# Experts stage: GpSimd issues the gathers of the tile two ahead in front of the accumulating transfers, from the last tile of 512 on

## The chip, the cores and the metric

The kernel runs on one core of one Trainium2 chip. The metric is the device time of one execution in microseconds (us). It is read from the median of three runs. The core has five engines that each run their own list of instructions in order and meet at semaphores: TensorE (PE, with its weight loads as PEld), VectorE (DVE), ScalarE (ACT), GpSimd (POOL) and SyncE (SP), and 16 DMA engines that carry all transfers.

## The reference

One decoder layer on x of 16 sequences by 256 tokens by 256, in float32. Three parts follow one another, each added to its input and normalised: a linear attention with decay, a cross attention over a context of 77 rows, and a mixture of experts. Only the last one matters here:

```
x = layernorm(x + ffn(x))          # the layer's last step, 4096 tokens of 256

probs = softmax(xf @ router_w.T)   # 8 experts
probs = probs * (top 2 of them)    # and divided by their sum
g = xf @ gate_w[e] + gate_b[e]     # 256 -> 512, per expert e
u = xf @ up_w[e] + up_b[e]
h = silu(g) * u
y = sum over e of probs[e] * (h @ down_w[e] + down_b[e])   # 512 -> 256
```

## The kernel before

The kernel runs five stages, with a barrier behind each: linear_attention, cross_attention, route_tokens, run_experts, combine. The routing stage gives every pair of a token and one of its two experts a slot, sorted by expert. The slots are cut into tiles, each with a single expert: 16 big tiles of 512 slots (BIGS = 16, tiles 0 to 15), then 7 half tiles of 256 (tiles 16 to 22), 23 in all (TILES). A tile is handled in blocks of 128 rows: 4 blocks in a big tile, 2 in a half tile. The last half tiles are the same code with 256 columns.

In run_experts each engine walks over the tiles with its own function tile(t, par, turn), where par is t % 2 and picks one of two buffers, and turn is t // 2. Tiles 0 and 1 are written out, tiles 2 to 13 run in a hardware loop (there t is a register, not an int), and 14 to 22 are written out again (all_tiles, L1779). What one tile does, by engine:

- SyncE (L1827) loads the weights of tile t + 2 into gu_raw and dn_raw, 0.5 MB each for gate, up and down, once the low parts of tile t are made, and the biases of t + 1.
- GpSimd (L1880) does three things in order. low_parts(t + 1) waits until ScalarE has made gu_hi of tile t + 1 and subtracts it from the first half of the raw weights to give that half of gu_lo. add_rows(t - 1) waits until the output rows of t - 1 are scaled (y_scaled) and until the accumulating transfers of t - 2 have landed (y_stored), then issues one indirect DMA per block that adds y_out to rows of sum_dram. gather_rows(t + 2) waits for index_ready of t + 2 and issues one indirect DMA per block that fetches the token rows into x_in.
- TensorE (L2122) begins a tile when x_lo and both halves of gu_lo for it are there. It multiplies by gate and up for f = 0 and 1 of the four blocks of 128 hidden columns (gate_up), then does the down projection of tile t - 1 (down), then turns the gathered rows of tile t + 1 (turn_x, which waits for x_loaded, the gathers), then f = 2 and 3. Each product is three matmuls, since both operands are split into a high and a low part.
- ScalarE (L1914) makes gu_hi of t + 1 from the raw weights, the gates with silu, the scaled output rows of t - 1 (scale_y), xT_hi of t + 1 from the turned rows, dn_hi and hid_hi.
- VectorE (L2025) makes hid, keeps the rows of t - 1 (keep_y, which waits for the accumulating transfers of t - 3 through y_stored), makes the other half of gu_lo of t + 1 (gu_low_last, L1997), xT_lo (x_low), the shares of t + 1 (shares), and then the index of tile t + 2 (tile_index, L2019), which waits for turn_x and shares of tile t. So index_ready of t + 2 comes behind x_low of t + 1, and that behind the transposes of t + 1.

The order on GpSimd is written out by hand in tile; there is no planner. Both kinds of indirect DMA are issued by GpSimd's instruction stream.

Of the kernel before, what the change touches and what calls it, by code (L numbers as in the profile page):

```python
# [1462 lines left out]
class Plan:  # L1463
# [29 lines left out]
    def blocks(self, t):  # L1493

        return (self.T if not isinstance(t, int) or t < self.BIGS else self.HALF) // P

    def first_block(self, t):

        if not isinstance(t, int) or t <= self.BIGS:
            return t * (self.T // P)  # L1500
        return (self.BIGS * self.T + (t - self.BIGS) * self.HALF) // P
# [203 lines left out]
def run_experts(nc, sh, plan, ident, x2_dram, slot_col, slot_row, counts, expert_of, tile_table, gate_w, gate_b, up_w, up_b, down_w, down_b, sum_dram):  # L1705
# [8 lines left out]
    T, BIGS, TILES = plan.T, plan.BIGS, plan.TILES  # L1714
# [5 lines left out]
    with ExitStack() as ctx:  # L1720
# [58 lines left out]
        def all_tiles(eng, tile):  # L1779

            for t in range(2):
                tile(t, t, 0)
            with eng.Fori(1, (BIGS - 2) // 2) as i:
                for par in range(2):
                    tile(2 * i + par, par, i)
            for t in range(BIGS - 2, TILES):
                tile(t, t % 2, t // 2)

        def has(t, ahead):

            return not isinstance(t, int) or 0 <= t + ahead < TILES
# [59 lines left out]
        @block.gpsimd  # L1851
        def _(pool):

            def gather_rows(t, par, turn):
                pool.wait_ge(index_ready[par], turn + 1)
                pool.sem_inc(pool_turns, 1)
                for blk in range(blocks(t)):
                    pool.indirect_dma_start(x_in[par][:, blk, :], None, x2_dram,  # L1858
                                            bass.IndirectOffsetOnAxis(index[par][:, blk:blk + 1], 0))\
                        .then_inc(x_loaded[par], 16)  # L1860

            def low_parts(par, turn):
                pool.wait_ge(gu_hi_done[par], turn + 1)
                pool.sem_inc(pool_turns, 1)
                for cols in (slice(0, FF), slice(FF, 2 * FF)):
                    ins = pool.tensor_tensor(gu_lo[par][:, 0, cols], gu_raw[par][:, 0, cols],
                                             gu_hi[par][:, 0, cols].bitcast(F32), ALU.subtract)
                ins.then_inc(gu_lo_done[par], 1)

            def add_rows(t, par, turn):  # L1870
                pool.wait_ge(y_scaled, first_block(t + 1))
                pool.wait_ge(target_ready, t + 1)
                if has(t, -1):
                    pool.wait_ge(y_stored[1 - par], 16 * plan.blocks_of_parity(t - 1, turn - 1 + par))
                pool.sem_inc(pool_turns, 1)
                for blk in range(blocks(t)):
                    pool.indirect_dma_start(sum_dram, bass.IndirectOffsetOnAxis(target[par][:, blk:blk + 1], 0),  # L1877
                                            y_out[par][:, blk, :], None, compute_op=ALU.add).then_inc(y_stored[par], 16)

            def tile(t, par, turn):  # L1880
                if has(t, 1):
                    low_parts(1 - par, turn + par)
                if has(t, -1):
                    add_rows(t - 1, 1 - par, turn - 1 + par)
                if has(t, 2):
                    gather_rows(t + 2, par, turn + 1)

            gather_rows(0, 0, 0)
            gather_rows(1, 1, 0)
            all_tiles(pool, tile)  # L1890
            add_rows(TILES - 1, (TILES - 1) % 2, (TILES - 1) // 2)

# [406 lines left out]
```

## Time and profile before

| | us |
|---|---|
| median of 3 runs | 1451.87 |
| the three runs | 1449.99, 1451.87, 1453.0 |
| the profiled execution | 1452.94 |
| its span, first to last instruction | 1450.9 |
| TensorE busy | 1315.6 (91%) |
| TensorE weight loads busy | 1115.7 (77%) |
| ScalarE busy | 953.5 (66%) |
| VectorE busy | 833.1 (57%) |
| GpSimd busy | 745.7 (51%) |
| mean granted TensorE clock | 0.953 |

The profile is of one execution. Busy times are sums over instructions, and a matmul's end is modelled, so a busy TensorE is not TensorE at its peak. Times within the span are counted from its first instruction. PEclk is the clock that the chip granted to TensorE, as a share of full speed. A releaser is what ended an engine's idle time, inferred from semaphores. The first gather of the experts stage starts at 1030.0 and the last accumulating transfer at 1417.2; the combine stage follows from 1423.3 to the end. "Landing" is the time from the start of the instruction that issues a transfer to its completion.

### The profile page before, as it was taken

The numbers are of one execution on the slowest core, as the hardware profiler recorded it, in microseconds if no ns is written. First come the engines' busy times: TensorE is split into PE (matmuls) and PEld (weight loads), VectorE is DVE, ScalarE is ACT, GpSimd is POOL, SyncE is SP. The second block draws the span as 40 slices with busy tenths as digits, with TensorE's granted clock in tenths as the row PEclk, the third lists the DMA queues.
The fourth block names the chain that finished last, engine by engine and source line by source line (L and its number), as shares of the span: only waits on it lengthen the run. The fifth ranks groups of instructions, "written<-read, shape, count | busy, mean of one in ns | idle before, by whom it ended". The sixth has DMA issues, their size and how long they took to land. (4 is left out here: it accounts for less than half of the span.)

```text
span 1450.9 us, 31123 instructions
## 1 busy us (share of the span) xinstructions
PE 1315.6 (91%) x10437; PEld 1115.7 (77%) x10437; DVE 833.1 (57%) x1707; ACT 953.5 (66%) x2168; POOL 745.7 (51%) x841
## 2 busy tenths in 40 slices
PE   5899999999999999999988999982599999999780
PEld 4788888888888888888876777761488888888680
DVE  3345554445454455544556888857366666666564
ACT  4577767777777777777745777772466666656553
POOL 2244443444444444443547777740357777776753
PEclk9999999999999999999999999995599999999895
DMA  3300100001000100010023343422346666666737
GB/s 138 82 9 30 31 23 25 21 23 31 23 31 16 30 24 30 24 37 9 23 80 86 107 104 98 112 83 72 113 136 153 153 155 154 155 157 163 180 78 239
DMA packets 136851, 117.54 MB, mean 81 GB/s; under 512 B 46578, under 2 KB 121690, under 8 KB 136730
## 3 DMA queue, kind: packets, MB, share of 16 engines
q1 hardware_dynamic: 121754, 95.36, 21.6%
q0 software_dynamic: 14976, 20.62, 8.1%
q8 instruction: 70, 1.15, 0.3%
q14 instruction: 51, 0.42, 0.1%
HBM read 79.89 MB, written 33.58 MB: 78 GB/s over the span
## 5 line engine op out<-in xcount | busy, mean ns | idle before, releaser
L345 POOL TENSOR_SCALAR_AFFINE_SELECT a_decay<-a_decay 128x256 f32<-128x256 f32 x256 | 115.2, 454 | 258.2 <-ACT a_decay L433 256.7
L565 DVE TENSOR_TENSOR a_probs<-a_ps_s,a_decay 128x384 f32<-128x384 f32 x256 | 131.6, 552 | 158.5 <-PE a_ps_o L752 147.4
L354 POOL TENSOR_TENSOR a_key_sum<-a_probs 128x256 f32<-128x256 f32 x128 | 94.5, 738 | 169.9 <-DVE a_probs L565 157.9
L1877 POOL DMA_INDIRECT sum_rows<-e_y_out,e_target x78 | 125.8, 1613 | 81.0 <-ACT e_y_out L1931 56.5
L396 ACT ACTIVATE a_qk_exp<-a_ps_qk 128x512 f32<-128x512 f32 x128 | 76.5, 598 | 137.2 <-PE a_ps_qk L658 130.0
L658 PE MATMUL a_ps_qk<-a_xT_hi,a_w_hi 128*128 128x256 f32 x512 | 144.8, 283 | 3.6 <-ACT a_qk_relu L397 3.6
L658 PE MATMUL a_ps_qk<-a_xT_hi,a_w_lo 128*128 128x256 f32 x512 | 143.8, 281 | 0.0
L658 PE MATMUL a_ps_qk<-a_xT_lo,a_w_hi 128*128 128x256 f32 x512 | 143.7, 281 | 0.0
L558 DVE SCALAR_TENSOR_TENSOR a_qk<-a_qk_exp,a_qk_relu 128x512 f32<-128x512 f32 x128 | 89.1, 696 | 94.5 <-ACT a_qk_relu L397 94.3
L733 PE MATMUL a_ps_s<-a_qk 64*128 64x256 f32 (+1 forms) x1024 | 132.2, 338 | 0.6 <-DVE a_probs L565 0.5
L431 ACT ACTIVATE a_decay<-a_ps_c,a_c_now 128x256 f32<-128x256 f32 x256 | 124.4, 486 | 2.1 <-PE a_ps_c L723 1.2
L1858 POOL DMA_INDIRECT e_x_in<-x_rows,e_index x78 | 81.1, 1039 | 79.1 <-DVE e_index L2023 56.0
L746 PE MATMUL a_ps_o<-a_probs,a_values 128*64 128x256 f32 (+1 forms) x1024 | 111.5, 339 | 0.4 <-DVE a_probs L565 0.4
L733 PEld LDWEIGHTS a_ps_s<-a_qk 64*128 64x128 f32 x1024 | 107.8, 187 | 2.5 <-issue 2.4
L658 PEld LDWEIGHTS a_ps_qk<-a_xT_hi,a_w_hi 128*128 128x128 f32 x512 | 97.8, 191 | 5.7 <-issue 5.6
L433 ACT ACTIVATE a_decay<-a_ps_c,a_c_now 128x128 f32<-128x128 f32 x256 | 98.4, 385 | 0.0
L658 PEld LDWEIGHTS a_ps_qk<-a_xT_hi,a_w_lo 128*128 128x128 f32 x512 | 98.0, 191 | 0.0
L658 PEld LDWEIGHTS a_ps_qk<-a_xT_lo,a_w_hi 128*128 128x128 f32 x512 | 97.8, 191 | 0.0
L359 POOL TENSOR_TENSOR a_oT_lo<-a_oT,a_oT_hi 128x256 fp32r<-128x256 f32 x128 | 94.4, 738 | 1.2 <-ACT a_oT_hi L450 1.2
L746 PEld LDWEIGHTS a_ps_o<-a_probs,a_values 128*64 128x64 f32 x1024 | 62.2, 136 | 41.5 <-issue 11.3
L1036 POOL TENSOR_TENSOR b_probs<-b_probs,b_top 128x1232 f32<-128x1232 f32 x32 | 72.7, 2273 | 39.8 <-DVE b_top L1231 39.8
L2119 PE MATMUL e_ps_y<-e_dn_hi,e_hid_hi 128*128 128x256 f32 x312 | 89.0, 285 | 3.1 <-DVE e_hid_lo L2039 2.2
(318 smaller groups left out, 4017.2 us busy)
## 6 DMA issues: line engine op xcount, KB each, us to landing
e_gu_raw<-in_L_ffn_gate_w SPq DMA_DIRECT2D x23, 512.0 KB
e_gu_raw<-in_L_ffn_up_w SPq DMA_DIRECT2D x23, 512.0 KB
e_dn_raw<-in_L_ffn_down_w SPq DMA_DIRECT2D x23, 512.0 KB, 5.3
a_x_in<-in_x SPq DMA_DIRECT2D x16, 256.0 KB, 2.7
a_x_res<-in_x SPq DMA_DIRECT2D x16, 256.0 KB
x_rows<-a_x SPq DMA_DIRECT2D x16, 256.0 KB, 2.2
x_bo_rows<-a_x_bo SPq DMA_DIRECT2D x16, 256.0 KB, 2.2
b_x_bo<-x_bo_rows SPq DMA_DIRECT2D x16, 256.0 KB, 2.9
```

The lines of the kernel that those rows point to most:

```text
L345: pool.affine_select(out=d, in_=d, compare_op=ALU.is_ge, fill=0.0, base=0, pattern=[[0, 2], [1, P]], channel_multiplier=-1)\
L354: pool.tensor_tensor(key_sum[:], probs[:, :, P:N], probs[:, :, N:TRI], ALU.add).then_inc(keys_summed, 1)
L359: pool.tensor_tensor(oT_lo[g % 2][:], oT[g % 2][:], oT_hi[g % 2][:].bitcast(F32), ALU.subtract).then_inc(oT_lo_done, 1)
L431: act.activation(decay[h][:, 0:N], ps_c[:, h, :], ACT.Exp, bias=c_now[:, 0, head:head + 1], scale=-1.0)
L433: act.activation(decay[h][:, N:TRI], ps_c[:, h, P:N], ACT.Exp, bias=c_now[:, 1, head:head + 1], scale=-1.0).then_inc(decay_exp[h], 1)
L558: vec.scalar_tensor_tensor(qk[g][:], qk_exp[:], 1.0, qk_relu[:], ALU.min, ALU.add).then_inc(qk_done, 1)
L565: vec.tensor_tensor(probs[:, h, :], ps_s[h][:, 0:TRI], decay[h][:], ALU.mult)\
L658: mm = pe.matmul(out, l, r, start=(n == 0), stop=(n == len(todo) - 1))
L733: mm = pe.matmul(ps_s[h][:, out], qk[g][rows, 1, j], qk[g][rows, 0, i], start=True, stop=True)
L746: pe.matmul(out[h][:, 0, cols], values[par][:, j, 2 * g + h, :], probs[:, h, keys], start=(j == 0), stop=(j == 1), skip_group_check=True)
L1877: pool.indirect_dma_start(sum_dram, bass.IndirectOffsetOnAxis(target[par][:, blk:blk + 1], 0), y_out[par][:, blk, :], None, compute_op=ALU ...
L2119: mm = pe.matmul(ps_y[n][:, 0:D], h[:, f, rows], w[par][:, f, :], start=(s == 0), stop=(s == len(todo) - 1))
```

## The change

In GpSimd's tile function the order of two calls depends on the tile. Up to tile 14 it stays as it was. In tiles 15 to 20 gather_rows(t + 2) stands in front of add_rows(t - 1). In tiles 21 and 22 there is nothing to gather. Nothing else is different: the same instructions with the same waits, and all other engines as before.

```diff
             def tile(t, par, turn):
                 if has(t, 1):
                     low_parts(1 - par, turn + par)
+                gathers_first = isinstance(t, int) and t >= BIGS - 1
+                if has(t, 2) and gathers_first:
+                    gather_rows(t + 2, par, turn + 1)
                 if has(t, -1):
                     add_rows(t - 1, 1 - par, turn - 1 + par)
-                if has(t, 2):
+                if has(t, 2) and not gathers_first:
                     gather_rows(t + 2, par, turn + 1)
```

## Rows read from the trace of the kernel before

**Rows 1.** Windows: us, busy by engine (instructions), PEclk granted clock, DMA share, GB/s

```profile
1283.00:1300.50 17.50, 17.50 (x105) 15.60 (x105) 11.19 (x20) 10.63 (x17) 12.94 (x10) 1.00 0.65 159
...
1342.30:1348.30 6.00, 0.00 (x0) 0.00 (x0) 1.56 (x2) 1.12 (x3) 4.76 (x5) 0.77 0.86 222
...
1348.30:1353.50 5.20, 5.17 (x29) 5.17 (x30) 2.08 (x8) 2.10 (x5) 4.05 (x3) 0.61 0.64 162
...
1368.90:1373.10 4.20, 0.04 (x1) 0.04 (x1) 2.99 (x2) 1.12 (x3) 4.03 (x3) 0.97 0.93 322
...
1373.10:1377.80 4.70, 4.70 (x28) 4.70 (x29) 1.81 (x7) 1.83 (x4) 2.75 (x3) 0.67 0.66 98
```

**Rows 2.** Waits of TensorE, 1300 to 1424: total us, times, longest us

```profile
PE e_ps_x L2096 <- DMA e_x_in<-x_rows,e_index: 12.6, 4, 6.0
```

**Rows 3.** Timeline of TensorE: start us, duration us, what [idle before <-releaser]

```profile
1332.92 0.33 PE L2096 MATMUL e_ps_x<-ident,e_x_in 128*128 128x128 f32 x1 [1.09 <-DMA e_x_in<-x_rows,e_index]
...
1348.33 1.12 PE L2096 MATMUL e_ps_x<-ident,e_x_in 128*128 128x128 f32 x4 [6.04 <-DMA e_x_in<-x_rows,e_index]
...
1353.48 0.28 PE L2107 MATMUL e_ps_g<-e_xT_hi,e_gu_hi 128*128 128x256 f32 x1
...
1362.91 0.36 PE L2107 MATMUL e_ps_g<-e_xT_hi,e_gu_hi 128*128 128x256 f32 x1 [0.21 <-DVE e_hid L2033]
...
1373.06 1.12 PE L2096 MATMUL e_ps_x<-ident,e_x_in 128*128 128x128 f32 x4 [4.18 <-DMA e_x_in<-x_rows,e_index]
...
1394.64 0.33 PE L2096 MATMUL e_ps_x<-ident,e_x_in 128*128 128x128 f32 x1 [1.27 <-DMA e_x_in<-x_rows,e_index]
...
1398.01 0.29 PE L2107 MATMUL e_ps_g<-e_xT_hi,e_gu_hi 128*128 128x256 f32 x1
```

**Rows 4.** Timeline of GpSimd, tiles 16 to 19

```profile
1333.91 1.62 POOL L1877 DMA_INDIRECT sum_rows<-e_y_out,e_target  x1 [2.32 <-ACT e_y_out L1931]
...
1339.71 1.56 POOL L1877 DMA_INDIRECT sum_rows<-e_y_out,e_target  x1 [0.30 <-issue]
...
1341.57 1.01 POOL L1858 DMA_INDIRECT e_x_in<-x_rows,e_index  x1 [0.30 <-issue]
...
1342.88 1.86 POOL L1858 DMA_INDIRECT e_x_in<-x_rows,e_index  x1 [0.31 <-issue]
...
1344.77 2.48 POOL L1866 TENSOR_TENSOR e_gu_lo<-e_gu_raw,e_gu_hi 128x512 fp32r<-128x512 f32 x2
...
1367.31 0.98 POOL L1858 DMA_INDIRECT e_x_in<-x_rows,e_index  x1 [0.30 <-DMA sum_rows<-e_y_out,e_target]
...
1368.32 2.50 POOL L1866 TENSOR_TENSOR e_gu_lo<-e_gu_raw,e_gu_hi 128x512 fp32r<-128x512 f32 x2
...
1376.93 1.01 POOL L1858 DMA_INDIRECT e_x_in<-x_rows,e_index  x1 [1.64 <-DVE e_index L2023]
```

**Rows 5.** Timeline of VectorE

```profile
1335.28 0.21 DVE L2023 CAST e_index<-e_token 128x2 uint32<-128x2 f32 x1
...
1359.78 1.22 DVE L2000 TENSOR_TENSOR e_gu_lo<-e_gu_raw,e_gu_hi 128x1024 fp32r<-128x1024 f32 x1
...
1369.27 2.65 DVE L2000 TENSOR_TENSOR e_gu_lo<-e_gu_raw,e_gu_hi 128x1024 fp32r<-128x1024 f32 x1
...
1374.90 0.75 DVE L1984 TENSOR_TENSOR e_xT_lo<-e_ps_x,e_xT_hi 128x256 fp32r<-128x256 f32 x2 [2.98 <-ACT e_xT_hi L1911]
...
1375.89 0.17 DVE L2023 CAST e_index<-e_token 128x2 uint32<-128x2 f32 x1
```

**Rows 6.** Timeline of ScalarE

```profile
1333.61 0.65 ACT L1911 CAST e_xT_hi<-e_ps_x 128x256 fp32r<-128x256 f32 x2 [0.57 <-PE e_ps_x L2096]
```

**Rows 7.** Landing times of the gathers, then of the accumulating transfers, whole span

```profile
DMA to landing us min/median/max: 2.7/3.9/6.9
...
DMA to landing us min/median/max: 3.6/4.9/7.5
```

**Rows 8.** Timeline of SyncE's queue

```profile
1365.23 0.39 SPq L1812 DMA_DIRECT2D e_gu_raw<-in_L_ffn_gate_w  x1
```

## The prediction

> **What bounds the kernel now.** I read the page's busy shares and its forty slices first. TensorE is busy 91% of the span, at full granted clock nearly everywhere, except in one slice near the middle and one near the end. The change touches only GpSimd's order from the last tile of 512 (tile 15) to tile 20, so I went to the windows of that stretch. In the steady big tiles TensorE has no gap: 17.50 us of 17.50, GpSimd 12.94 [rows 1]. Among the half tiles it falls to nothing for 6.0 us and again for 4.2 us, and the stretches behind these gaps run at a granted clock of 0.61 and 0.67 [rows 1]. The table of waits gives one releaser for nearly all of it: the transposes of e_x_in wait for the gather, 12.6 us in 4 waits [rows 2]. The timeline places them: 1.09 us before the rows of tile 17, 6.04 before 18, 4.18 before 20, 1.27 before 22 [rows 3]. The chain of waits is no help here, since it goes back only to the last stage, which starts at a barrier; whatever TensorE saves before that barrier moves it by as much.
>
> Why the gathers come late is seen on GpSimd. Index 18 was ready at 1335.28 + 0.21 = 1335.49 [rows 5], but its gathers started only at 1341.57, directly behind four accumulating transfers that began at 1333.91 [rows 4]. The second gather started at 1342.88 and TensorE moved at 1348.33, so it took 5.45 us to land [rows 3, 4]. For tile 20 it is a smaller queue (two transfers) and a slow landing: 1367.31 to 1373.06, 5.75 us, just when 1.5 MB of weights are issued, from 1365.23 [rows 3, 4, 8].
>
> **What the stalls cost together.** A transposition that doesn't lose the clock is followed by the next tile's first matmul after 1398.01 - 1394.64 = 3.37 us; behind the 6.04 us gap it took 1353.48 - 1348.33 = 5.15 [rows 3], that is 1.78 more. The 4.18 us gap has the same tail: 1373.06 to 1377.8, 4.74, so 1.37 more [rows 1, 3]. In rows, the clock is granted at 0.61 and 0.67 of 2.4 GHz there, a mix of its levels of 1.2 and 2.4 GHz, after TensorE had done nothing for 6.0 and 4.2 us; gaps of 1.09 and 1.27 had no such tail. All that could come back is 12.6 + 1.8 + 1.4 = 15.8 us.
>
> **Part 1, the gathers move forward (tiles 17 to 22).** Nothing is added or removed: two gathers each for six tiles pass 16 accumulating transfers (four each for the rows of tiles 14 and 15, two each for 16 to 19). A gather that GpSimd waits for starts 0.87 us after its index (1375.89 + 0.17 to 1376.93), and the second starts 0.30 + 1.01 later [rows 4, 5]: 2.18 from index to second start. Its landing took 2.7 to 6.9 us, median 3.9 [rows 7]. From the transposes to the next index it is 1376.06 - 1373.06 = 3.0 [rows 3, 5]. So one round of gather, transposition and index lasts 2.18 + landing + 3.0, against a half tile on TensorE of 1362.91 - 1353.48 = 9.43 [rows 3]. A landing up to 4.25 us is hidden, each us above is paid once per tile. Tile 17 has a whole big tile as cover: its 1.09 goes.
>
> **Part 2, the transfers move back, and with them the low parts.** Behind a tile's transfers stands, on the same in-order engine, the subtraction that makes the first half of e_gu_lo for the next tile, and TensorE can't begin that tile without it. Tile 18 is where this decides. Index 18 gains what ScalarE idled before the cast of x 17, 0.57 of the 1.09 [rows 6]: 1335.49 - 0.57 = 1334.92. Then gathers: + 0.87 + 1.01 + 0.30 + 0.98 = 1338.08. Four transfers: + 0.30 + (1339.71 + 1.56 - 1333.91 = 7.36) = 1345.74. Low part: + 0.03 + 2.5 = 1348.3 [rows 4]. TensorE without any wait for rows would want it at 1348.33 - 6.04 - 1.09 + 3.37 = 1344.6 [rows 3]. So of the 6.04 us a wait of 3.7 comes back in another place (a gather that lands by 1348.3 - 3.37 = 1344.9, 7.8 us after the second one's start, is hidden in it), and tile 18 begins at 1348.4 instead of 1353.48: 5.1 saved. A gap of 3.7 us stands nearest to the one of 4.18, so I charge its tail too, 1.4. Bounds for that tail: nothing (as behind 1.27 us) and 1.8. That puts tile 19 at 1348.4 + 1.4 + 9.43 = 1359.2 instead of 1362.91.
>
> **Part 3, tiles 19 to 22.** GpSimd's own round is now: index, 0.87, gathers 2.29, 0.30 and two transfers (about 3.4, from singles of 1.56 to 1.62 with 0.30 between), then the low part 2.5: 9.4 us, as long as TensorE's 9.43 [rows 3, 4]. It has no slack, and one gather took 1.86 in place of 1 us [rows 4]. I take 9.6 per tile: three rounds from 1359.2 end at 1388.0, where tile 22 now begins at 1398.01. That is 10.0 us. The ends of a round are 9.43 (nothing stretched, median landing) and 10.6 (landings as 18's, 5.45): tile 22 at 1387.5 or 1391.0, a gain of 10.5 or 7.0; with the tail of part 2 free, 11.9.
>
> **What the moved transfers could hold up.** They land 3.6 to 7.5 us after issue [rows 7]. VectorE waits for those of tile t-2 before it writes the rows of t, which is more than a tile later. GpSimd waits for the previous tile's before the next: the last of tile 15's starts at 1345.74 - 1.56 = 1344.2 and has landed by 1351.7 at worst, where tile 16's come up at 1348.3 + 0.30 + 2.29 + 0.30 = 1351.2. That costs nothing, since the low part of 19 would end at 1351.2 + 3.4 + 2.5 = 1357.1, with 2 us to spare before 1359.2. After tile 20 the order is as before, and the tail from tile 22 on, the barrier and the last stage are unchanged.
>
> **The skill's rule on the shared port.** The subtraction on VectorE that makes the other half of e_gu_lo took 1.22 us alone, but 2.65 at 1369.27, ending 1.1 us after GpSimd's low part at 1368.32 + 2.50 [rows 4, 5]. The Trainium skill, "SBUF — State Buffer", section "SBUF: two separate sides", says that VectorE with two SBUF inputs and a GpSimd instruction that reads SBUF exclude each other for a whole instruction, the first to start winning. The trace agrees with it in this place. It speaks against this change, which puts the low part where VectorE's own piece falls due. By this rule, were the low part always first, the time would be the port rival's below; by the sum above it is not.
>
> **The rivals.** *All of it comes back* (about 15.8 us, 1436): would need the low part of 18 not to be late, though it stands behind 7.36 us of transfers. *Gathers still land late*: moved forward, they may still meet the weights, which in the row for tile 21 are issued at 1365.23, while index 20 + 0.87 would be only some 2 us earlier. Landings of 5.75 as for 20 make a round 10.9, tile 22 at 1391.9, gain 6: 1446. *The port decides*: if VectorE's piece queues behind the low part, index to index is 0.87 + 2.29 + 0.30 + 3.4 + 2.5 + 1.1 + 1.16 (from the low part of x at 1374.90 to the index at 1376.06 [rows 5]), 11.6; tile 22 at 1394.0, gain 4.0: 1448. For it, the 2.65 row; against, VectorE's piece would start just ahead of the low part in my schedule. *Slower*: GpSimd's wait for the previous tile's transfers sets the round, at landing + 0.87 + 1.86. To lose everything three rounds must exceed 1398.01 - 1359.2 = 38.8, a round 12.9, a landing 10.2. At 12 us, a round is 14.7 and tile 22 starts at 1403.3: 5.3 slower, 1457. For it speaks that transfers now fall under the weights, where the windows show DMA shares of 0.86 and 0.93 [rows 1]; against, that none took over 7.5 [rows 7]. *No change*: both of these together, rounds of 12 to 13.9 (three of them from 1359.2 end within 2.9 us of 1398.01), 1451.
>
> **How the numbers follow.** The profiled execution took 1452.94 us with a span of 1450.9, so 2.04 lie outside the span; it is 1.07 above the median of 1451.87, within the spread of the three runs (1449.99 to 1453.0). 10.0 off gives 1442.9 for that execution and 1441.9 for the median. Chances: forecast 0.58 (1439.5 to 1444.5), all back 0.10, gathers land late 0.15, port 0.07, no change 0.05, slower 0.05. The range 1437.0 to 1448.0 leaves out the far end of "all back", part of the port's case, and the last two. Faster by over 0.2% (2.9 us, about what can be told from nothing here) takes all but part of the port's case: 0.88; within it 0.07; slower 0.05.
>
> **What would show it.** Right: the waits of the transposes for the gathers fall from 12.6 to under 3 us; the gathers of 17 to 22 stand in front of the transfers, about 0.9 us behind their index; a new wait of TensorE or of its weight load for e_gu_lo of 2.5 to 4 us appears before tile 18, with a granted clock below full behind it; tiles 19 to 22 follow at 9.4 to 9.9 us. Wrong: landings of over 5 us in a row, several VectorE pieces of 2.6 us with x waiting behind them, or GpSimd idle in front of a transfer for y_stored.

## The result and the profile after

The changed kernel is slower: ratio 1.0023 to the kernel before, 95% interval 1.0015 to 1.0031 (medians 1455.92 and 1452.91 us, 16 runs each). That is 3.3 us more where I had forecast 10 us less. Measured again beside the experiments, the ratio was 1.0023 again (1.0010 to 1.0036, e9_changed_again). Its profiled execution took 1456.97 us with a span of 1455.2.

At tile 15 the two traces happen to stand at the same time. I use the last event there that the change can't touch as a zero: in tile 15 TensorE waits 0.87 us (0.86 in the changed kernel) for e_y_out and starts again, at 1313.58 before and 1313.57 after. From there to the end of the last down matmul it is 99.9 us before and 104.2 us after, so the whole difference (4.3 us between these two executions) arises in the half tiles.

The wait that the change was to remove is removed, and another is there. These are TensorE's waits from 1300 on (total us, times, longest us), where [rows 2] had 12.6 us for the gathers:

```profile
PE e_ps_g L2110 <- DVE e_hid L2036: 12.1, 5, 3.1
...
PE e_ps_x L2099 <- DMA e_x_in<-x_rows,e_index: 2.5, 1, 2.5
...
PE e_ps_y L2122 <- DVE e_hid_lo L2042: 2.2, 1, 2.2
```

The timeline of TensorE shows them one by one (start us, duration us, what, idle before and its releaser). It answers to [rows 3]: four gaps before, six now, at the first matmul of tiles 17 to 19, 21 and 22 and at the transposes of 20.

```profile
1337.09 0.36 PE L2110 MATMUL e_ps_g<-e_xT_hi,e_gu_hi 128*128 128x256 f32 x1 [2.02 <-DVE e_hid L2036]
...
1350.98 0.36 PE L2110 MATMUL e_ps_g<-e_xT_hi,e_gu_hi 128*128 128x256 f32 x1 [3.10 <-DVE e_hid L2036]
...
1362.99 0.35 PE L2110 MATMUL e_ps_g<-e_xT_hi,e_gu_hi 128*128 128x256 f32 x1 [1.22 <-DVE e_hid L2036]
...
1371.53 0.44 PE L2099 MATMUL e_ps_x<-ident,e_x_in 128*128 128x128 f32 x2 [2.55 <-DMA e_x_in<-x_rows,e_index]
...
1388.67 0.35 PE L2110 MATMUL e_ps_g<-e_xT_hi,e_gu_hi 128*128 128x256 f32 x1 [3.04 <-DVE e_hid L2036]
...
1402.13 0.35 PE L2110 MATMUL e_ps_g<-e_xT_hi,e_gu_hi 128*128 128x256 f32 x1 [2.69 <-DVE e_hid L2036]
```

Each half tile now has its own gap. The releaser of five of the six is VectorE's e_hid. The first matmul of a tile overwrites the product from which VectorE makes hid for f = 2 of the tile before, and in VectorE's list that hid stands behind the subtraction, x_low, the shares and the index, so it is late when one of these is. The next view is therefore VectorE's timeline (lines have moved by 3: L2003 is VectorE's own half of gu_lo, L2017 the share, L2026 the index, L1994 the target):

```profile
1332.14 3.31 DVE L2003 TENSOR_TENSOR e_gu_lo<-e_gu_raw,e_gu_hi 128x1024 fp32r<-128x1024 f32 x1
...
1347.02 3.11 DVE L2017 SCALAR_TENSOR_TENSOR e_share<-e_x_in,expert_of 128x2 f32<-128x2 f32 x1
...
1358.84 2.51 DVE L2003 TENSOR_TENSOR e_gu_lo<-e_gu_raw,e_gu_hi 128x1024 fp32r<-128x1024 f32 x1
...
1361.28 0.74 DVE L1987 TENSOR_TENSOR e_xT_lo<-e_ps_x,e_xT_hi 128x256 fp32r<-128x256 f32 x2
...
1362.26 0.17 DVE L2026 CAST e_index<-e_token 128x2 uint32<-128x2 f32 x1
...
1369.36 3.98 DVE L2003 TENSOR_TENSOR e_gu_lo<-e_gu_raw,e_gu_hi 128x1024 fp32r<-128x1024 f32 x1
...
1381.03 3.41 DVE L1994 CAST e_target<-e_token 128x2 uint32<-128x2 f32 x1
...
1394.22 3.78 DVE L1994 CAST e_target<-e_token 128x2 uint32<-128x2 f32 x1
```

Alone the first, the share and the target take 1.22 us (L2003), 0.21 (L2017) and 0.16 (L1994). Here the long ones last 3.31, 3.11, 2.51, 3.98, 3.41 and 3.78: one in each of the tiles 16 to 21, 15.9 us more than alone in sum. Before, there were two such, the 2.65 of [rows 5] and its like in tile 21. GpSimd's timeline says what runs beside them (the row at 1347.05 is the low part of 18, the one at 1357.19 that of 19, the one at 1369.21 that of 20; the last row is the gather of 22):

```profile
1347.05 3.06 POOL L1866 TENSOR_TENSOR e_gu_lo<-e_gu_raw,e_gu_hi 128x512 fp32r<-128x512 f32 x2
...
1351.28 1.10 POOL L1858 DMA_INDIRECT e_x_in<-x_rows,e_index  x1 [1.18 <-DVE e_index L2026]
...
1357.19 3.07 POOL L1866 TENSOR_TENSOR e_gu_lo<-e_gu_raw,e_gu_hi 128x512 fp32r<-128x512 f32 x2
...
1363.30 1.10 POOL L1858 DMA_INDIRECT e_x_in<-x_rows,e_index  x1 [3.04 <-DVE e_index L2026]
...
1366.24 1.62 POOL L1877 DMA_INDIRECT sum_rows<-e_y_out,e_target  x1 [0.30 <-issue]
...
1369.21 3.04 POOL L1866 TENSOR_TENSOR e_gu_lo<-e_gu_raw,e_gu_hi 128x512 fp32r<-128x512 f32 x2
...
1375.29 1.23 POOL L1858 DMA_INDIRECT e_x_in<-x_rows,e_index  x1 [3.04 <-DVE e_index L2026]
...
1388.97 1.10 POOL L1858 DMA_INDIRECT e_x_in<-x_rows,e_index  x1 [4.57 <-DVE e_index L2026]
```

The low part of 19 ends at 1357.19 + 3.07 = 1360.26 and VectorE's piece, issued at 1358.84, ends at 1361.35, 1.1 us later, just as in the one case of [rows 4, 5]. Behind it come x_low and the index at 1362.43, and 0.87 later the gather at 1363.30. So index waits for low part (through VectorE's held piece), low part for transfers, transfers for gathers, gathers for index: a ring of 12.0 us (1351.28 to 1363.30, and 1363.30 to 1375.29), where TensorE needs 9.43. Only these two rounds are that short: from the gather of 18 (at 1337.39) to that of 19 it is 13.9 us, and from 1375.29 to 1388.97 it is 13.7. TensorE's three rounds from the start of tile 19 to that of 22 take 1402.13 - 1362.99 = 39.1 us, 13.0 each.

The held pieces don't make up every gap. The low part of 18 itself ends only at 1347.05 + 3.06 = 1350.11, behind its four transfers, and TensorE had been idle since 1350.98 - 3.10 = 1347.88. So 2.2 of the 3.10 us before tile 18 are the price of the queue that part 2 of the prediction names, and the held share adds the rest. The low parts of 17, 19, 21 and 22 end before TensorE falls idle; there it is the held piece. The wait of 2.55 us for the gathers of 20 ends 6.8 us after the second of them was issued (1364.70).

The clock adds to it. Windows of the gaps before tiles 18 and 21 and of the work behind them (us, busy by engine, granted clock, DMA share, GB/s):

```profile
1347.90:1351.00 3.10, 0.02 (x1) 0.05 (x1) 3.06 (x5) 0.14 (x1) 2.20 (x2) 1.00 0.51 71
...
1351.00:1355.50 4.50, 4.50 (x25) 4.50 (x26) 3.36 (x7) 3.22 (x5) 3.61 (x3) 0.63 0.89 296
...
1385.60:1388.70 3.10, 0.06 (x2) 0.06 (x1) 2.35 (x8) 2.76 (x8) 0.00 (x0) 1.00 0.17 40
...
1388.70:1393.30 4.60, 4.60 (x26) 4.60 (x27) 3.36 (x7) 3.22 (x5) 3.72 (x3) 0.63 0.21 63
```

Behind the gaps of 3.10 and 3.04 us, and those of 2.02, 2.55 and 2.69, the granted clock is 0.62 to 0.66 for some 4.5 us, a mix of the levels 1.2 and 2.4 GHz. Behind the gap of 1.22 it is not: there the 24 matmuls before the down projection take 2.95 us, behind 3.10 they take 4.31. Five gaps lost 1.2 to 1.5 us each this way. Before, two did, and so did the 2.18 us wait before the last down projection: it cost 1.3 there and nothing in the trace of the changed kernel, though the wait is the same.

### The profile page after: what moved, and what is told of

It reads as the page before. It is cut to its first block and busy times, and to the rows that moved or that the text cites. A ratio compares the mean times of both kernels' runs of the same rounds, so it can differ in the third digit from the quotient of the medians.

```text
span 1455.2 us, 31123 instructions
## 1 busy us (share of the span) xinstructions
PE 1318.2 (91%) x10437; PEld 1119.2 (77%) x10437; DVE 846.1 (58%) x1707; ACT 952.6 (65%) x2168; POOL 744.1 (51%) x841
## 5 line engine op out<-in xcount | busy, mean ns | idle before, releaser
L558 DVE SCALAR_TENSOR_TENSOR a_qk<-a_qk_exp,a_qk_relu 128x512 f32<-128x512 f32 x128 | 89.1, 696 | 94.6 <-ACT a_qk_relu L397 94.4
L746 PEld LDWEIGHTS a_ps_o<-a_probs,a_values 128*64 128x64 f32 x1024 | 62.2, 136 | 41.4 <-issue 11.4
```

The source lines that it names most:

```text
L558: vec.scalar_tensor_tensor(qk[g][:], qk_exp[:], 1.0, qk_relu[:], ALU.min, ALU.add).then_inc(qk_done, 1)
L746: pe.matmul(out[h][:, 0, cols], values[par][:, j, 2 * g + h, :], probs[:, h, keys], start=(j == 0), stop=(j == 1), skip_group_check=True)
```

## The experiments

The ratios are those to the kernel before on the same chip, with 95% intervals; the medians of the kernel before beside the experiments were 1456.4 to 1456.8 us (1452.9 beside the first measurement of the changed kernel), so 0.001 is 1.46 us. The last column is the length of the stretch from the zero of above to the last down matmul's end in the profiled execution; it is free of the drift of several us that the earlier stages show from one execution to the next, but it is of one execution, and the gaps differ from one to the next: the ratio decides. The edits below are shortened to the lines that matter.

| kernel | ratio | interval | stretch, us |
|---|---|---|---|
| before | 1 | | 99.9 |
| changed, and e9_changed_again | 1.0023 both | 1.0015 to 1.0031; 1.0010 to 1.0036 | 104.2; 105.0 |
| e1_fill | 0.9959 | 0.9944 to 0.9974 | 94.5 |
| e2_low_on_vector | 0.9935 | 0.9920 to 0.9949 | 96.2 |
| e3_before_low_on_vector | 1.0017 | 1.0006 to 1.0027 | 102.6 |
| e4_low_between | 0.9964 | 0.9951 to 0.9978 | 94.6 |
| e5_stand_in_reads | 1.0025 | 1.0013 to 1.0038 | 106.0 |
| e6_stand_in_fills | 0.9969 | 0.9955 to 0.9983 | 95.1 |
| e7_low_in_gap | 0.9922 | 0.9907 to 0.9938 | 90.9 |
| e8_only_tile_16 | 0.9996 | 0.9986 to 1.0007 | 98.9 |
| e10_low_16_too | 0.9938 | 0.9925 to 0.9951 | 91.4 |

Two theories stood against each other. **Port:** VectorE's instructions with operands in SBUF are held until GpSimd's subtraction ends. **Queue:** GpSimd simply reaches the low part too late behind the transfers, and TensorE waits for it.

**e1_fill**

```diff
-    ins = pool.tensor_tensor(gu_lo[par][:, 0, cols], gu_raw[par][:, 0, cols], gu_hi[par][:, 0, cols]...)
+    ins = pool.memset(gu_lo[par][:, 0, cols], 0.0)     # and one memset of 1536 columns ahead, tiles 17 to 22
```

> The changed kernel, in which GpSimd's low parts of tiles 17 to 22 (1024 columns subtracted, 2.5 us, two operands read from SBUF) are replaced by memsets of 2560 columns (about 2.4 us by the memsets of the first stages, 1280 columns in 1.16 us), which read nothing; the first half of gu_lo of those tiles is zero, so the output leaves that part out. Theory of the port (VectorE's instructions with SBUF operands are held until GpSimd's low part ends): the six VectorE instructions of 2.5 to 4.0 us shrink to their 0.2 or 1.22 us, and the time falls by 8 to 14 us against the changed kernel, to about 1442 to 1448. Theory of the queue (GpSimd only reaches the low part too late, behind the transfers): GpSimd's list is as long as before, so the time stays at 1455 to 1457.

Measured 0.9959, that is 0.64% or 9.3 us below the changed kernel, at nearly equal length of GpSimd's step (2.9 us against 3.1). That is what the port theory said, in size and direction. But the queue's share shows too, in the waits of TensorE:

```profile
PE e_ps_g L2121 <- POOL e_gu_lo L1875: 3.2, 1, 3.2
...
PE e_ps_x L2110 <- DMA e_x_in<-x_rows,e_index: 3.5, 3, 2.4
```

The 3.2 us wait before tile 18 is my predicted 3.7. The subtractions of VectorE were 1.22 us throughout; two casts were held, for 2.59 and 2.14 us.

**e2_low_on_vector and e3_before_low_on_vector**

```diff
# GpSimd
-    if has(t, 1):
+    if has(t, 1) and not (isinstance(t, int) and t >= BIGS):
         low_parts(1 - par, turn + par)
# VectorE, behind gu_low_last(1 - par, turn + par)
+    if isinstance(t, int) and t >= BIGS:
+        vec.tensor_tensor(gu_lo[1 - par][:, 0, :], gu_raw[1 - par][:, 0, :], gu_hi[1 - par][:, 0, :]...).then_inc(gu_lo_done[1 - par], 1)
```

> The changed kernel, with the low parts of tiles 17 to 22 made wholly by VectorE (one more subtraction of 1.22 us per half tile right behind its own), none by GpSimd. Both theories: no instruction of GpSimd that reads SBUF is left in the half tiles and nothing stands behind the transfers, so 1441 to 1446; the added 1.2 us of VectorE per tile costs up to 1.2 x 6 = 7 us if x_low stands right behind it. If neither theory holds (the gathers or the weights set the pace), 1455.

> The kernel before (transfers in front of gathers) with the same move of the low parts to VectorE: it tells what the order alone is worth once the port is free. Port theory: the gathers of 18 still wait for four transfers, so TensorE's 6 us before 18 stay and some of the 4.2 before 20 go: 1449 to 1453, that is 5 to 10 us slower than e2_low_on_vector. Queue theory the same. If the order of the gathers isn't worth anything, equal to e2_low_on_vector.

With the low parts off GpSimd the two orders differ by 0.82%, 12 us: that is what the order of the gathers is worth when nothing else moves (my 10 was near it). Moving the low parts under the old order doesn't help and costs 0.17%: the 6 us before 18 stay, with 13.3 us of waits for gathers in all, and VectorE has 1.2 us more per tile. Neither edit alone gains; both together do, by 0.65% (9.5 us). That the 12 is near my 10 is in part chance: my sum held 3.7 us of wait for the low part of 18 and a lost clock behind it, and in e2 no low part stands behind the transfers.

**e5_stand_in_reads and e6_stand_in_fills**

```diff
 # e2, and in GpSimd's tile where the low part stood (no engine waits for it)
+    pool.wait_ge(gu_hi_done[par], turn + 1)
+    for k in range(2): pool.tensor_tensor(scratch[:, k, :], scratch[:, 2, :], scratch[:, 2, :], ALU.subtract)   # e5
+    for k in (3, 2):   pool.memset(scratch[:, 0:k, :], 0.0)                                                     # e6
```

> As e2_low_on_vector, but where GpSimd's low part stood in tiles 16 to 21 it now does a stand-in of the same form (two subtractions of 512 columns on scratch space, 2.5 us), for which no engine waits. Port theory: VectorE's instructions with operands in SBUF that fall beside it are held until it ends, 1 to 3 us each, nearly one per half tile, so the time goes back from e2's 0.9935 of the kernel before to 0.998 to 1.003. Queue theory: TensorE waited for gu_lo itself, and it doesn't any more, so 0.993 to 0.996 (only the next gathers can be late by some tenths).

> The twin of e5_stand_in_reads: the stand-in is two memsets of 1536 and 1024 columns (about 2.5 us, reading nothing). Both lists of GpSimd are equally long, so the queue theory expects the same time for both. Port theory: the subtractions of VectorE aren't held; its casts (index and target) may be, as one was for 2.59 and one for 2.14 us in e1_fill: 0.993 to 0.997, at least 3 us faster than e5.

This pair isolates the port, since TensorE's operands come from VectorE in both. 1.0025 against 0.9969: 8.2 us, although e6's stand-in is the longer one (2.98 against 2.60 us). VectorE in e5, and GpSimd in e5 beside it:

```profile
1339.14 2.80 DVE L2017 TENSOR_TENSOR e_gu_lo<-e_gu_raw,e_gu_hi 128x1024 fp32r<-128x1024 f32 x1
...
1354.35 3.34 DVE L2040 CAST e_index<-e_token 128x2 uint32<-128x2 f32 x1
...
1364.62 2.42 DVE L2008 CAST e_target<-e_token 128x2 uint32<-128x2 f32 x1
...
1377.16 3.29 DVE L2008 CAST e_target<-e_token 128x2 uint32<-128x2 f32 x1
...
1390.61 3.17 DVE L2008 CAST e_target<-e_token 128x2 uint32<-128x2 f32 x1
```

```profile
1338.25 2.60 POOL L1877 TENSOR_TENSOR e_scratch<-e_scratch 128x512 f32<-128x512 f32 x2
...
1355.03 2.62 POOL L1877 TENSOR_TENSOR e_scratch<-e_scratch 128x512 f32<-128x512 f32 x2
...
1364.43 2.58 POOL L1877 TENSOR_TENSOR e_scratch<-e_scratch 128x512 f32<-128x512 f32 x2
...
1377.82 2.59 POOL L1877 TENSOR_TENSOR e_scratch<-e_scratch 128x512 f32<-128x512 f32 x2
...
1391.16 2.58 POOL L1877 TENSOR_TENSOR e_scratch<-e_scratch 128x512 f32<-128x512 f32 x2
```

The subtraction of 1339.14 ends at 1341.94, 1.09 us behind the stand-in (1340.85); the casts, recorded from up to 0.7 us ahead of a stand-in or just behind its start, end with it to 0.04 us. A sixth piece, a subtraction in tile 21, took 2.18. VectorE and GpSimd in e6:

```profile
1369.90 1.22 DVE L2017 TENSOR_TENSOR e_gu_lo<-e_gu_raw,e_gu_hi 128x1024 fp32r<-128x1024 f32 x1
...
1391.55 2.60 DVE L2008 CAST e_target<-e_token 128x2 uint32<-128x2 f32 x1
```

```profile
1369.72 2.98 POOL L1877 MEMSET e_scratch<- 128x1536 f32 x2
...
1392.16 2.98 POOL L1877 MEMSET e_scratch<- 128x1536 f32 x2
```

The same subtraction takes 1.22 us right beside a memset, while a cast is still held, for 2.60. Three casts are held in e6 (1.88, 2.59 and 2.60 us), and one subtraction, queued behind the second of them, took 1.82 and ended with it. e6 lies 0.34% above e2; the held casts and the 3 us more in GpSimd's list per tile both stand for it, and no run separates them.

**e4_low_between**

```diff
 # GpSimd from tile 16 on; for tile 15's rows two of four transfers go ahead of the low part
     gather_rows(t + 2, par, turn + 1)
-    add_rows(t - 1, 1 - par, turn - 1 + par)
+    low_parts(par, turn + 1)          # of t + 2, no longer at the next tile's start
+    add_rows(t - 1, 1 - par, turn - 1 + par)
```

> Nothing left out. From tile 16 on GpSimd does the gathers of t + 2, then the low part of t + 2 as soon as ScalarE's high part is there, then the transfers of t - 1 (for tile 15's rows two of the four ahead of the low part). Port theory: the low part of the next tile now runs in front of VectorE's own piece instead of beside it, so most of the held instructions go, and the time is 1443 to 1450. Queue theory: the low parts come 4 us earlier, the transfers later: 1443 to 1450 as well. If late transfers hold the kernel (VectorE's or GpSimd's wait for y_stored), 1456 or slower.

0.9964, as both theories had it. Its trace bears the port out in part: from tile 18 on no VectorE subtraction is held, in tiles 16 and 17 two are, 3.29 and 4.05 us. Against the changed kernel it gains 0.59% with the same instructions on the same engines. How much of that comes from the reading step missing VectorE's pieces, and how much from the low part no longer standing behind the transfers, this run doesn't tell.

**e8_only_tile_16**

```diff
-    gathers_first = isinstance(t, int) and t >= BIGS - 1
+    gathers_first = isinstance(t, int) and t == BIGS
```

> The change in one tile alone: only in tile 16 do the gathers (of 18) go ahead of the four transfers. The 6 us before 18 go; GpSimd's low part of 18 ends near 1348.3 to 1350, so TensorE waits 3 to 5 us for it or for VectorE held beside it. Port theory: one or two VectorE instructions held there, the rest as in the kernel before with its stall of 4 us for 20: 0.996 to 1.000. Queue theory: tile 18 begins at 1348.4, 5 us earlier than before, and the rest as before: 0.996.

0.9996, no change that can be measured: inside the port's range, outside the queue's as I wrote it. It doesn't decide between the two. Four VectorE pieces are held here, three of them from tile 18 on (2.62, 2.02 and 2.02 us), which is more than I expected of the port; but the wait for the gathers of 19 is new too, 1.7 us, and these stand behind the late low part in GpSimd's own list. Its waits show part 2 of the prediction nearly as written:

```profile
PE e_ps_x L2099 <- DMA e_x_in<-x_rows,e_index: 7.6, 4, 3.3
...
PE e_ps_g L2110 <- POOL e_gu_lo L1866: 3.8, 1, 3.8
```

The 6 us before 18 have become 3.8 us for GpSimd's gu_lo, with the clock lost behind it. TensorE's waits for the gathers of 17, 19, 20 and 21 come to 7.6 us, against 1.09 + 4.18 + 1.27 = 6.5 for 17, 20 and 22 in [rows 3], and those for e_hid to 1.4 against 0.4: what the one gap gave, the others took.

**e7_low_in_gap and e10_low_16_too**

```diff
 # e2's edit of GpSimd; VectorE's added piece stands here instead
     hidden(0)
     hidden(1)
+    if has(t, 1) and isinstance(t, int) and t >= BIGS:       # e10: t >= BIGS - 1, GpSimd's edit too
+        vec.wait_ge(gu_hi_done[1 - par], turn + par + 1)
+        vec.tensor_tensor(gu_lo[1 - par][:, 0, :], gu_raw[1 - par][:, 0, :], gu_hi[1 - par][:, 0, :]...)
     keep_y(t - 1, 1 - par, turn - 1 + par)
```

> Nothing left out. The order of the changed kernel with the low parts of tiles 17 to 22 on VectorE, the first half not behind VectorE's own piece (as in e2) but ahead of the kept rows, where VectorE idles 0.6 to 0.9 us and ScalarE's high part is already there. If the four waits of TensorE for e_hid of 1.1 us in e2 come from x_low standing behind the added piece, they shrink and the time is 2 to 4 us below e2: 0.991 to 0.993. If they come from the gathers, the same as e2.

> e7_low_in_gap with the low part of tile 16 on VectorE as well. In all kernels so far the cast of the target in tile 15 took 1.93 us beside GpSimd's low part of 16, and TensorE waited 0.87 us for the kept rows behind it. Port theory: that wait goes, and the time is 0.5 to 1 us below e7 (0.9915 to 0.992). Rival (the wait comes from the rows of a big tile, four blocks through two banks): no difference.

e7 has the lowest ratio: 0.9922, 11.4 us below the kernel before and 14.7 below the changed one (1.0023 - 0.9922). Its interval overlaps those of e2 (0.9935) and e10 (0.9938), so among the three no best one is shown. TensorE's waits in it:

```profile
PE e_ps_g L2115 <- DVE e_hid L2036: 5.3, 6, 1.7
...
PE e_ps_x L2104 <- DMA e_x_in<-x_rows,e_index: 0.9, 1, 0.9
```

The time is in the expected range, but not by the expected way: the waits for e_hid were to shrink from e2 and grew, from 3.8 to 5.3 us, while those for the gathers fell from 5.8 to 0.9. From tile 16 on no VectorE instruction is held, and no gap is over 1.8 us, save the 2.18 before the last down projection. In e10 the 1.93 us cast of tile 15 went back to 0.16 and TensorE's wait behind it from 0.87 to 0.23:

```profile
1316.50 0.39 PE L2127 MATMUL e_ps_y<-e_dn_hi,e_hid_hi 128*128 128x256 f32 x1 [0.23 <-DVE e_y_out L1998]
```

So the low part had held the cast, and the wait came from there, as expected. The time didn't follow: 0.9938 lies outside the expected 0.9915 to 0.992, with an interval that overlaps e7's. A gain of 0.6 us (0.0004) can't be seen in intervals that are 0.003 wide.

e9_changed_again is in the table:

> The changed kernel itself, beside the kernel before on the chip of this call, so that the ratios of the experiments stand against one of their own. Both theories: 1.0015 to 1.0031, as at first, and in the trace each of the tiles 16 to 21 has one VectorE instruction held for 2.5 to 4 us.

Its trace has six VectorE instructions held from tile 16 on, one per tile as in the first one, at 2.67 to 4.05 us. They aren't all the same ones: in tile 17 it is a piece of hid_lo (3.24 us, 0.42 alone), again a subtraction of two SBUF operands. Before tile 18 TensorE waited 4.2 us for GpSimd's gu_lo itself, so there the queue made the whole gap.

## Why the prediction was wrong

The predicted range (1437.0 to 1448.0) and the direction were wrong.

**What held.** The bound was read rightly: 12.6 us of waits for gathers, gone to 2.5. The gather starts 0.87 us behind its index wherever GpSimd waits for it (part 1). The queue's price at tile 18, 3.7 us with a lost clock behind it, is there as 3.2 in e1, 3.8 in e8 and 4.2 in e9, and as 2.2 of the 3.10 us in the changed kernel's first trace. The other thing I checked, transfers waiting for transfers, cost nothing in the changed kernel. And e2 against e3 gives 12 us for the order, once the low parts are off GpSimd.

**The step that failed** is part 3, "GpSimd's own round is now [...] 9.4 us, as long as TensorE's 9.43", with the sentence that put the port aside: "VectorE's piece would start just ahead of the low part in my schedule." I had the row that speaks against it and the mechanism, priced at 11.6 us a round, and gave it 0.07. The ring took 12.0 us in its two shortest rounds, and TensorE's rounds from tile 19 to 22 came to 13.0 each, where I had taken 9.6. No number stood behind "just ahead". In the trace they came within 0.15 us of each other in tile 19 (1369.36 and 1369.21), the low part first. As I read the traces, once that has happened the ring keeps itself in place: the held piece delays index and hid, so that TensorE stops, VectorE's next pieces come later, and one of them (subtraction, share or target cast) again falls beside the next low part. A margin of some tenths between starts that long chains on two engines set was no reason against a rival.

**The price was too low as well.** I let the port act in three rounds, from tile 19 on, and only through VectorE's subtraction. It acted from tile 16 on and through share and casts too. So tile 18 began at 1350.98, not 1348.4, and tile 19 at 1362.99, 3.8 us after my 1359.2; the three rounds behind it took 39.1 us against the rival's 34.8, 4.3 more. These 8.1 us bring the rival's 1448 to 1456. And I charged one clock loss, while five gaps of 2.0 to 3.1 us each lost 1.2 to 1.5. In the balance of the two traces, from zero to end: waits in the stretch before the last down projection 13.0 us before and 14.6 after, + 1.6; clock tails 4.5 and 6.8, + 2.3; together 3.9 of the 4.3 us. The 0.4 left isn't assigned.

**The rivals.** "The port decides" was right in its mechanism, and its 1448 was too low by the 8.1 us above. "Gathers still land late" came true for one tile: those of 20 landed 6.8 us after the second was issued, where the rival had 5.75, and cost 2.55 us and 1.4 of clock. "Slower" by transfers that wait for transfers didn't occur: no gap of TensorE is released by them.

Not separated: how much of the 9.3 us between the changed kernel and e1 is the held instructions themselves and how much the clock that goes with the gaps. Nor, in the changed kernel as it stands, the port's share from the queue's: in e5 and e6 no engine waits for what GpSimd computes, so their 8.2 us are the port's, but they are measured there. And the 2.5 us wait for the gathers of 20 stays in the changed kernel as in e1 and e2; whether the weights' transfers cause it wasn't tried.

## What to carry to other kernels

Before moving a GpSimd instruction that reads SBUF, list which VectorE instructions with SBUF operands will run beside it in the new order, and price each collision as the full rest of GpSimd's instruction. One lengthened row in the trace of before was reason enough to expect it in every tile. A freed wait on an in-order engine is worth its length only if what stands behind the moved work isn't due next; here the order (12 us) paid only once the low parts were off GpSimd. Count how many gaps remain, not just their sum: each gap of 2 to 3 us may cost the clock, which one of 6 us had cost once. Five did here, but others of that length in other runs didn't (see below), so it is a range in the sum and not a fixed term.

## What the runs showed of the hardware

A VectorE cast (float32 to uint32, 2 columns, 0.16 us alone) is held by GpSimd's memsets as well, 2.60 and 2.59 us in e6 and e1, while a subtraction of two SBUF operands is not. The Trainium skill, "SBUF — State Buffer", section "Who interferes with whom", has both: copies and casts may contend in their two-port modes, the subtraction only with a GpSimd instruction that reads. The traces agree on what is held and what isn't; they don't show in which mode the cast ran.

The other direction, VectorE holding up GpSimd, is in the traces too. In the changed kernel GpSimd's issue of one accumulating transfer took 2.42 us instead of 1.56, with VectorE's subtraction of 1.22 us beside it:

```profile
1325.67 2.42 POOL L1877 DMA_INDIRECT sum_rows<-e_y_out,e_target  x1 [0.30 <-issue]
```

```profile
1325.44 1.22 DVE L2009 TENSOR_TENSOR e_dn_lo<-e_dn_raw,e_dn_hi 128x1024 fp32r<-128x1024 f32 x1
```

The 1.86 us gather of [rows 4] is of the same kind: VectorE's subtraction ran there from 1342.67, with 1.01 us left when the gather's issue began, and the issue took 0.88 longer. The lengthening follows what is left of the subtraction: in the changed kernel, in the rows above, 0.86 with 0.99 left, in e7 0.39 with 0.51 left (at 1388.81), in e4 1.03 with 1.10 left (at 1371.26). An issue that began ahead of the subtraction took about 0.3 more at most.

The Trainium skill, "SBUF — State Buffer", section "Who interferes with whom", infers that tensor_tensor leaves descriptor generation alone, because it takes only the read interface and descriptor generation needs the write one. For these indirect DMAs the measured rows say otherwise. Their issue also has to read the row numbers (e_index, e_target), and no run separates that reading from the writing of descriptors.

TensorE's granted clock fell behind the gaps of 2.02 to 3.10 us in the changed kernel's first trace and not behind 1.22 or 1.27. The length alone doesn't settle it. In e9_changed_again the clock stayed at 1.00 behind gaps of 2.02 and 2.43 us, in e5 behind 2.65 and in e8 behind 3.33; in e10 it was 0.62 behind a gap of 1.85 and in e5 behind 1.94:

```profile
1340.31:1344.80 4.49, 4.49 (x37) 4.49 (x38) 3.61 (x8) 3.62 (x6) 3.58 (x3) 1.00 0.62 231
...
1361.30:1365.80 4.50, 4.50 (x25) 4.50 (x26) 3.38 (x7) 3.25 (x5) 3.59 (x3) 0.62 0.29 78
```

The first row is e9_changed_again behind 2.02 us, the second e10 behind 1.85.
